# A gated state-space layer: set-up rebuilt, last chunk's outputs by quarters, 16 unused matmuls

## The reference

```python
xn = _layernorm(x)                        # outer norm
x_norm = _layernorm(xn, ln_in_g, ln_in_b) # inner norm
x_norm = x_norm + conv1d(x_norm, conv_w) + conv_b     # depthwise, 3 taps
gate, input_gate = split(x_norm @ gate_w.T + gate_b)
Bm = x_norm * sigmoid(input_gate) @ B_w.T + B_b
Cm = x_norm @ C_w.T + C_b
A_bar = expm(dt_A * A)
s = _layernorm(state @ A_bar + b_t, ln_st_g, ln_st_b) # 2048 times, in order
ssm = (Cm * s) @ D_w.T + D_b
out = x + ssm * sigmoid(gate) * silu(xn @ W.T + b + (xn @ V_r) @ C.T)
```

## Time and profile before

| | us |
|---|---|
| median of 3 runs | 2551.97 (2548.98 to 2552.64) |
| profiled execution, its own time | 2550.3 |
| its span | 2548.5 |
| TensorE busy | 2472.2 (97%) |
| VectorE busy | 2199.2 (86%) |
| GpSimd busy | 1270.9 (50%) |
| ACT busy | 1006.3 (39%) |

### The profile page before, as it was taken

One profiled execution on the slowest core, in us unless ns is written; L12 is line 12 of the kernel. 1 busy time (PEld: TensorE's weight loads), 2 busy tenths in 40 slices (PEclk: granted clock), 3 DMA queues, 4 the chain that ended last, 5 costly groups with the idle time before them and its releaser, 6 DMA issues.

```text
span 2548.5 us, 42474 instructions
## 1 busy us (share of the span) xinstructions
PE 2472.2 (97%) x10001; PEld 1303.5 (51%) x10001; DVE 2199.2 (86%) x10937; ACT 1006.3 (39%) x1834; POOL 1270.9 (50%) x2480
## 2 busy tenths in 40 slices
PE   6899999999999999999999999999999999999986
PEld 3445555555555555555555555555555555555543
DVE  4688898888899888898888899888899888899876
ACT  3343344434344434334444334444344444334310
POOL 1355554455555455555455555455555455555442
PEclk8899999999999999999999999999999999999997
DMA  3111121221121221121222121122111122112112
GB/s 109 24 42 42 40 53 47 54 59 42 40 55 49 51 59 42 40 57 47 51 58 49 40 50 50 47 58 57 38 44 51 49 56 59 41 40 54 31 37 52
DMA packets 99798, 125.19 MB, mean 49 GB/s; under 512 B 32159, under 2 KB 48735, under 8 KB 99552
## 3 DMA queue, kind: packets, MB, share of 16 engines
q1 hardware_dynamic: 98912, 121.43, 19.5%
q10 hardware_dynamic: 640, 1.05, 0.1%
HBM read 71.96 MB, written 33.55 MB: 41 GB/s over the span
## 4 chain that ended last, share of the span: by engine, by line
POOL 48%; DVE 33%; issue 13%; PE 3%; ACT 0%; POOLq 0%; DVEq 0%; DMA 0%; ACTq 0%; SPq 0%
POOL dw L352 43%; DVE wq L760 14%; DVE dw L771 9%; DVE dw L785 9%; POOL ln L374 5%; PE bank L996 1%; PE bank L936 0%; ACT z L422 0%; PE bank L1029 0%; POOLq L223 0%; PE bank L987 0%; POOL ln L376 0%; PE bank L1061 0%; POOL ln L378 0%; POOL ln L377 0%
## 5 line engine op out<-in xcount | busy, mean ns | idle before, releaser
L352 POOL TENSOR_TENSOR dw<-q,minus_half 8x1 f32<-8x1 f32 x2048 | 1101.7, 538 | 1185.7 <-DVE wq L760 1154.9
L1029 PEld LDWEIGHTS bank<-Mscan,wT 128*65 128x65 f32 x2046 | 218.3, 136 | 660.2 <-issue 652.9
L987 PE MATMUL bank<-xnorm,gateT 128*128 128x512 f32 x1024 | 508.2, 595 | 0.0
L760 DVE SCALAR_TENSOR_TENSOR wq<-dw 8x65 f32<-8x65 f32 x2048 | 443.7, 217 | 70.3
L996 PE MATMUL bank<-xnorm,gateT 128*128 128x512 f32 x1024 | 502.7, 598 | 1.1 <-issue 1.1
L979 PE MATMUL bank<-xnT,WT 128*128 128x512 f32 x1024 | 495.7, 595 | 0.0
L1029 PE MATMUL bank<-Mscan,wT 128*65 128x128 f32 x2046 | 408.3, 281 | 33.3 <-DVE wT L788 24.9
L1030 PE MATMUL bank<-Mscan,wT 128*65 128x128 f32 x2046 | 393.3, 274 | 0.0
L785 DVE SCALAR_TENSOR_TENSOR dw<-dw 8x64 f32<-8x64 f32 x1024 | 280.1, 273 | 121.3 <-POOL dw L352 90.6
L771 DVE SCALAR_TENSOR_TENSOR dw<-dw 8x64 f32<-8x64 f32 x1024 | 281.1, 275 | 89.9 <-POOL dw L352 82.7
L775 DVE SCALAR_TENSOR_TENSOR dw<-bank,dw 8x128 f32<-8x128 f32 x1024 | 342.7, 335 | 8.9 <-PE bank L1030 8.0
(11 more groups left out here) (140 smaller groups left out, 2745.9 us busy)
## 6 DMA issues: line engine op xcount, KB each, us to landing
xc<-in_x SPq DMA_DIRECT2D x264, 128.0 KB, 2.7
out<-o SPq DMA_DIRECT2D x256, 128.0 KB, 2.4
xa<-in_x SPq DMA_DIRECT2D x248, 128.0 KB, 2.7
dw<-dtok SPq DMA_DIRECT2D x128, 96.0 KB
wtok<-dw SPq DMA_DIRECT2D x128, 33.0 KB
gateT<-in_gateT SPq DMA_DIRECT2D x1, 2048.0 KB
xa<-in_x ACTq DMA_DIRECT2D x8, 128.0 KB, 3.7
WT<-in_WT SPq DMA_DIRECT2D x1, 1024.0 KB, 6.0
```

The source lines that it names most:

```text
L352: nc.gpsimd.tensor_tensor(dw[0:B, t, CR:CR + 1], q[:], minus_half[0:B, 0:1], ALU.pow).then_inc(s["r_ready"], 1)
L760: V.scalar_tensor_tensor(out=wq[:], in0=w_eps, scalar=1.0 / S, in1=w_eps, op0=ALU.mult, op1=ALU.mult, accum_out=q[:]).then_inc(s["q_ready" ...
L987: ins = mm(mbank["gate", m][:], gateT[:, k, P * m:P * m + P], xnorm[p][:, k, :], start=(k == 0), stop=(k == KH - 1))
L1029: mm(scanP[0:WIDE, 0:2 * S], wT[:, 0:WIDE], Mscan[:, 0, :], start=True, stop=False)
```

## The change

Set-up:
- SP loads the edges and chunk 0 of batches 4 to 7 only; ACT loads VT and CrT (the factors of the low-rank product) first and then the edges and chunk 0 of batches 0 to 3.
- TensorE starts with the four W' products, into four banks instead of two; then come 4 matmuls of the identity with itself, and one more behind each of the 12 series matmuls: 16 whose result nobody reads (`keep_busy`).
- VectorE adds W' behind squarings 0 to 3. Other tables are spread anew: halo transposes behind squarings 0 to 3, z of chunk 0 behind 4, 6, 8, 10, taps behind 8 to 15, input gate from 10 on and by k first, with its own banks, x transposes behind 17 and 19. b_proj is behind the last squaring among the matrix products, and c_proj behind `fill_d`.
- The halo's normalised tiles go to o instead of z, so that ACT normalises halo and chunk 0 one behind the other, and then copies the halo. y and the centre tap alternate by k.
- GpSimd's `ln_op` for n < 3 does the four columns' power as one operation (7 and 5 operations instead of 13 and 8).
- The statistics of chunk 1 (n = 2) end behind the set-up's last VectorE copy.

Last chunk (`LAST` = 31): the gate products stand at steps 25 to 40 instead of 30 to 45. Its outputs are made by quarters of 16 time steps (q = 0 to 3): q = 0 to 2 between the steps 42 to 63, q = 3 behind the scan. A quarter has one transpose of w, an affine of 128 columns, `last_states` (128 columns), `last_mm` (4 products of 128 columns), `last_gated` (two halves of two pieces of 128 columns), `last_fill_o` (4 transposes), `last_sum` (two halves) and one DMA of 256 KB. x is loaded again by quarters early in that chunk.

The diff, cut to its core:

```diff
-PE_GATE_LAST = range(30, 46)
-V_G_LAST = (37, 38, 41, 42, 49, 50, 53, 54)
-PE_HALO = (0, 0, 1, 1)
-PE_Z0 = (2, 2, 3, 3)
-PE_WPRIME = (4, 5, 10, 11)
-DVE_WPRIME = (9, 10, 12, 13)
-DVE_CONV = (4, 5, 6, 7)
-PE_IG0 = (8, 8, 9, 9, 10, 10, 11, 11, 12, 12, 13, 13, 14, 14, 15, 15)
-PE_X0 = (10, 10, 12, 12)
-DVE_XG0 = (11, 13, 15, 17)
-DVE_STATS2 = (14, 15, 16, 17)
-PE_B0 = (14, 16, 17, 18)
-PE_C0 = (17, 18, 19, 19)
+PE_GATE_LAST = range(25, 41)
+V_G_LAST = (30, 31, 34, 37, 38, 41, 42, 45)
+LAST = NC - 1
+PE_W_LAST = (42, 43, 53)
+PE_SSM_LAST = (48, 50, 57)
+PE_O_LAST = (52, 54, 61)
+V_YS_LAST = (46, 49, 56)
+V_SG_LAST = (50, 51, 52, 53, 59, 60)
+V_ADD_LAST = (54, 55, 57, 58, 62, 63)
+PE_HALO = (0, 1, 2, 3)
+PE_Z0 = (4, 6, 8, 10)
+DVE_WPRIME = (0, 1, 2, 3)
+DVE_CONV = (8, 10, 12, 14)
+IG0 = tuple((m, k) for k in range(KH) for m in range(3)) + tuple((3, k) for k in range(KH))
+PE_IG0 = (10, 11, 12, 12, 13, 14, 14, 15, 16, 16, 17, 18, 18, 19, 20, 20)
+PE_X0 = (17, 17, 19, 19)
+DVE_XG0 = (18, 19)
+DVE_STATS2 = (17, 18, 19)
...
+            pe.wait_ge(s["vc_in"], 16 * 2)
+            for k in range(KH):
+                mm(wbank[k][:], VT[:, P * k:P * k + P], CrT[:], start=True, stop=True).then_inc(s["wprime_mm"], 1)
             pe.wait_ge(s["consts"], 16 * 4)
+
+            def keep_busy(n):
+                for _ in range(n):
+                    mm(banks[7][:, 0:P], ident[:], ident[:], start=True, stop=True)
+
+            keep_busy(4)
...
                 mm(scanP[0:S, 0:S], As[:, 1, :], XX[:, 0, :], start=True, stop=True
                    ).then_inc(s["pe_setup"], 1)
+                keep_busy(1)
...
+                whole = lambda a, b: g.tensor_tensor(b, a, minus_half[:], ALU.pow)
+                ins = (first + [
+                    lambda: whole(both, rr),
+                    lambda: g.tensor_tensor(bz, nm, rr, ALU.mult),
+                    lambda: whole(a, r1),
+                    lambda: g.tensor_tensor(bx, nm, r1, ALU.mult),
+                ] if n < 3 else first + [
...
+                for m in range(KH):
+                    ins = mm(last_ssm[q][:, P * m:P * (m + 1)], DT[:, P * m:P * (m + 1)], ys[:, P * q:P * (q + 1)],
+                             start=True, stop=True)
+                ins.then_inc(s["last_ssm"], 1)
...
+            def send_last(q):
+                wait_for(sp, "last_add", 2, q, 2)
+                hold(sp)
+                sp.dma_start(out[:, CT * LAST + QT * q:CT * LAST + QT * (q + 1), :], z[:, q, :]
+                             ).then_inc(s["last_out"], 16)
...
-            iteration(NC, "C", False)
+            send_last(0)
+            send_last(1)
+            send_w(LAST, NQ - 1)
+            send_last(2)
+            send_last(3)
```

More of the change, by code:

```diff
@@ L239, in wait_bank, with load_ends, quarter, of_rows @@
                     return
+        def load_ends(eng, b):
+            p0 = CT * (b % BJ)
+            ends = x[b, :, :].rearrange("(m r) h -> m r h", r=CT)[:, 0:CT:CT - 1, :]
+            eng.dma_start(xc[p0:p0 + CT, b // BJ, :], ends).then_inc(s["halo_in"], 16)
+        def quarter(a, q):
+            return a.rearrange("p (b q t) -> p q b t", b=B, q=NQ)[:, q]
+        def of_rows(a):
+            return a.rearrange("p (b t) -> p b t", b=B)
+        last_p = LAST % 2
+        last_w = [banks[5 + q % 2] for q in range(NQ)]
+        last_ssm = [banks[4 + 3 * (q % 2)] for q in range(NQ)]
+        last_o = [banks[1 + q % 2] for q in range(NQ)]
         block = ctx.enter_context(nc.Block())
@@ L525, in state_affine @@
                 a_(bank, bank, ACT.Identity, bias=sm("st_b"), scale=sm("st_g")).then_inc(s["sn_done"], 1)
-            for b in range(B):
+            for dst, src in [(VT[:], VT_d), (CrT[:], CrT_d)]:
+                act.dma_start(dst, src).then_inc(s["vc_in"], 16)
+            for b in range(B // 2):
+                load_ends(act, b)
+            for b in range(B // 2):
                 p0 = CT * (b % BJ)
@@ L628, in _ @@
             iteration(NC - 1, 1, "FC")
-            iteration(NC, 0, "C")
+            for q in range(NQ):
+                if q == 0:
+                    wait_for(act, "wrfill", 1, LAST, 0)
+                wait_for(act, W_IN[q], 16, LAST, 16)
+                a_(wr[:, q, 0:S], wtok[:, q, CD:CD + S], ACT.Copy,
+                   scale=wtok[:, q, CR:CR + 1]).then_inc(s["last_wr"], 1)
+                wait_for(act, "last_wT", 1, q, 1)
+                bank = last_w[q][0:S, 0:P]
+                a_(bank, bank, ACT.Identity, bias=sm("st_b"), scale=sm("st_g")).then_inc(s["last_sn"], 1)
         @block.vector
@@ L878, in _ @@
             assert done[0] == SETUP_M
+            for h in range(2):
+                gated_x(0, 2, h, 0)
             dve.wait_ge(s["pe_setup"], SQ_END + 1)
@@ L885, in _ @@
             link(V.tensor_copy(dw[0:B, CT - 1, CM:CM2], scanP[0:B, 3 * S:4 * S]))
+            for h in range(2):
+                gated_x(0, 3, h, 0)
             dve.wait_ge(s["pe_setup"], SQ_END + 2)
@@ L890, in _ @@
             assert done[0] == SETUP_END
+            for h in range(2):
+                bn_stats(2, NJ - 1, h)
+            aggregate(2)
             def iteration(i, p, parts):
@@ L923, in _ @@
             iteration(NC - 1, 1, "FC")
-            iteration(NC, 0, "C")
+            last_states(3)
+            for h in range(2):
+                last_gated(3, h)
+            for h in range(2):
+                last_sum(3, h)
         @block.tensor
@@ L1099, in _ @@
             pe.wait_ge(s["dve_setup"], SETUP_END)
+            for k in range(KH):
+                c_proj(0, k, 0, -1, False)
             def iteration(i, p, parts, middle):
```

196 lines of the change are left out of this document (141 added, 55 removed).

## The result

| | before | after |
|---|---|---|
| median | 2550.92 (2548.98 to 2552.64, 4 runs) | 2531.85 (2531.44 to 2532.26, 4 runs) |
| ratio, 95% interval | | 0.9923 (0.991 to 0.9936) |
| profiled span | 2548.5 | 2529.6 |
| mean granted clock | 0.985 | 0.994 |

The sum is close because its terms missed in both directions, which is luck. I cut both profiled executions at the same four points: the scan's first step, the start of chunk 31, the end of the last power, the end of the span.

The account below looks back on a forecast made before the run. The prediction took the serial chain over GpSimd's power and VectorE as the bound. Set-up -15.5, first steps +1.5, last chunk +1.0 and tail -8.4 gave -21.4 us on the median 2551.97: 2530.6 us, range 2520 to 2541.

Parts of the forecast that it names:

- Set-up, -15.5: Before the scan: its first step was to come at 75.5 us instead of 90.98, 15.5 us earlier.
- so I let it rise inside the third product, at 9 to 10: Set-up: TensorE's clock was to rise to 2.4 GHz within the third W' product, at 9 to 10 us.
- I cost them at nothing: Set-up series: the other 12 unused matmuls were to hide in TensorE's 0.43 us waits; uncovered they would cost 3 us.
- The page against the row: Set-up: the skill's page keeps squarings 0 to 10 slow, as forecast; a row's clock rise at 28 allows them fast.
- First steps, +1.5: Scan's first steps: VectorE waiting for the look-ahead was to lose 3.5 us instead of 2.0, costing 1.5 (0 to 4).
- Last chunk, +1.0: Last chunk: earlier gates save 2.2 us, outputs by quarters add more; plus 1.0 in all (-1.5 to +3).
- plus 3.2 for the outputs by quarters: Last chunk: 2.0 us of VectorE pieces, 2.2 of TensorE products, transposes and fills, 0.2 more, less 1.2 for overlap and clock.
- Tail, -8.4: Behind the last power: 9.4 us of computing plus 3.3 for the output DMA, 12.7 instead of 21.1; minus 8.4.
- (a): Unused matmuls and early W' keep TensorE at 2.4 GHz through series, halo fills and gates; 2525 us, chance 0.20.
- (b): Set-up: ACT's serial run and late statistics bind, scan starts at 82, first steps lose 5; 2538.6 us, chance 0.25.
- (c): Set-up: unused matmuls do nothing or cost their 3 us uncovered; 2533 us, chance within the forecast's 0.50.
- (d): GpSimd's 128x4 power, four times in series, makes it slower than before from 6.9 us on; chance 0.02.

Follow-up runs that it names:

- e1: The changed kernel without its 16 unused matmuls; 2526.91 us, ratio 0.9921.
- e4: The changed kernel with the set-up's 128x4 powers as four 128x1 operations each; 2530.98 us, one time only.
- e3: The kernel before with only the new last chunk and tail; 2542.93 us, ratio 0.9969.
- e12: The kernel before with only the last chunk's gates moved earlier (TensorE steps 25 to 40, VectorE 30 to 45); 2550.36 us, ratio 0.9989.
- e2: The changed kernel's set-up with the old last chunk and old tail; 2538.79 us, ratio 0.9961.
- e10: The changed kernel run again without an edit; 2531.69 us, ratio 0.9923.
- e6: The changed kernel without unused matmuls and with W' formed over 128 rows, zero-padded, instead of 32; 2524.92 us, one time only.
- e11: The changed kernel with two unused products behind each series term instead of one; 2539.55 us, ratio 0.9953.
- e8: The changed kernel without the set-up's unused matmuls, with three of 128x512 behind the scan's last look-ahead; 2524.59 us, one time only.
- e7: The changed kernel without the set-up's unused matmuls, with three of 128x512 behind c_proj; 2527.37 us, one time only.
- e9: The changed kernel without its 16 unused matmuls, W' over 128 rows, wide products behind c_proj and in the tail, last output in two halves; 2526.09 us, ratio 0.9899.
- e5: The changed kernel with its first four unused matmuls 512 columns wide, moving ones; 2535.59 us, one time only.

## Why the prediction was right in its sum and wrong in its terms

**Set-up, -15.5 against -9.6.** The step that failed is "so I let it rise inside the third product, at 9 to 10". W' ran for 7.2 us at the lower level, and the four unused matmuls took 2.08 instead of 1, so the series' first operation came at 12.39; that part cost little (12 had been forecast), since the loads landed at 3.26 and not at 5. The following sentence, "I cost them at nothing", is the larger miss: at 1.2 GHz an unused product with its load outlasts the 0.43 us of cover, and made a term 0.22 longer. The series went from 15.29 to 28.91, 13.6 us against 11.2 in e1, and ended 2.4 us behind the 26.5 of the forecast.

The 5.9 us add up like this. When the gates began 3.6 of them were there (46.08 instead of 42.5): the 2.4 of the series; 0.3 from its end to squaring 4 (7.3 us where 7.0 had been forecast, since squarings 0 to 3 took 1.66 each where I had 1.2, while the stall of 2 us at squaring 4 wasn't there: the fill at 36.85 stands right behind the squaring's passes); and 0.9 in squarings 4 to 10, which took 9.85. There the forecast's own terms give 9.85 and not 9: three squarings of 1.07 and four of 0.68 with a fill of 0.98, which hides their wait. The gate products and x's transposes took 22.8 us (to 68.92) where 21.1 had been added up. Their part at the lower clock, 4.3 us, was not longer than forecast. From there to the end of dtok's first copy (76.33) it was 7.4, where 7.5 had been forecast, and the DMA from that copy's end to the first step took 5.1 us where 4.4 had been read the earlier trace rows; SP's wait and issue are in both. The wide power, 1.04 instead of 1.5, was not on this path (e4).

**The page against the row.** The squarings 0 to 10 ran slow (0.47 and 1.11 for four transposes, until 46). The Trainium skill, "TensorE: Matmul & The Clock Gate", Part 4: PE-mode transpose, says that transposes don't engage full speed; here the trace agrees. The rise at 28 in the kernel before speaks against that rule as a general one. It stands in all three traces with the old set-up (28.3, and 29.2 and 28.8 in e3 and e12), which has eight transposes in a row where the new one has four, and no run here shows whether that is the reason.

**First steps, +1.5 against -2.5.** The order was read rightly: chunk 1's transposes do stand before the look-ahead. Two sizes were wrong. ACT's z ended 2.2 us behind the scan's start in the forecast (77.7 against 75.5) and 1.1 behind it in the trace (82.5 against 81.41). And the forecast had no term for the clock, which was still full there: c_proj (76.30 to 79.9), moved right in front of that gap, had run at the higher level. This isn't firm: e2, with the same set-up, took 78.34 for chunk 0, after and e10 76.29 and 76.45. That c_proj as such keeps the clock up is therefore not shown, only that VectorE waits 0.5 to 0.8 us for the look-ahead of step 2 with the clock up (six traces) and 1.9 to 2.4 with it down (e1, e2, e6, e11).

**Chunks 1 to 30.** They took 2.3 us longer without any edit. The powers had a mean of 541 ns against 538 before. e4, with the same middle chunks, had 538 again and 2278.1 us for the 30 chunks. Over all 14 traces, the four with a mean of 538 or 539 (before, e4, e6, e8) took 2278.1 to 2279.9, the ten with 540 or 541 took 2280.6 to 2282.4, the old set-up standing in both groups. So this goes with the execution, not with the change. Per chunk it is 0.08 us, so the 76.1 of the forecast held.

**Last chunk, +1.0 against -2.1.** The minus 2.2 for the wait was right (2.3 in e12). The plus 3.2 for the outputs by quarters came out as 0.25 in this execution and as up to 1.6 in others. Its parts don't close either: the VectorE pieces named are 6.0 us of work, and how they become 2.0 isn't said, and the 0.2 for the fills of w is counted twice. The 1.0 us at step 57 for TensorE's products was rightly seen, but it depends on the clock: the wait came where the clock had fallen by then (0.78 to 1.39 in e1, e3, e7, e9, e11), while in the changed kernel the clock was full from 2501 to 2511 and the longest wait was 0.35. I had also added VectorE's pieces to its steps one by one, but a step of the scan waits for GpSimd's power each time, and a short piece goes into that wait. The timeline of VectorE in the changed kernel shows two quarter pieces, a ys of 0.27 with 0.19 of wait left behind it and a sum of 0.41, in a pair of steps that took 2508.22 - 2505.85 = 2.37 us, no more than any other:

```profile
2505.85 0.27 DVE L871 SCALAR_TENSOR_TENSOR dw<-dw 8x64 f32<-8x64 f32 x1
...
2506.57 0.27 DVE L833 TENSOR_TENSOR ys<-bank,cT 64x128 f32<-64x128 f32 x1
2507.03 0.27 DVE L885 SCALAR_TENSOR_TENSOR dw<-dw 8x64 f32<-8x64 f32 x1 [0.19 <-POOL dw L401]
...
2507.82 0.41 DVE L855 TENSOR_TENSOR z<-bank,xa 128x256 f32<-128x256 f32 x1
2508.22 0.27 DVE L871 SCALAR_TENSOR_TENSOR dw<-dw 8x64 f32<-8x64 f32 x1
```

**Tail, -8.4 against -7.1.** The computing part was forecast at 9.4 and took 9.42, operation by operation. The output was under-sized: 4.6 us for one DMA of 256 KB where I took 3.3 from one of 128 KB. It was within the bounds (to 5), and e9 took 3.5 by halves.

**The rivals.** (a) did not happen, the clock stayed low. (b) named the right place for the wrong reason: the scan did start at 81.4, near its 82, but TensorE's series was late, not ACT; e4 shows ACT and GpSimd with 1.1 us to spare on the way to the scan's start. (c), the unused matmuls uncovered, is what happened; they cost 4.4 us to the gates' start and not 3, because the price had been worked out for the higher clock. (d) did not happen: the wide power took 1.04 us.

## What to carry to other kernels

- A filler matmul costs what it costs at the clock that it finds. Compare it, with its weight load and at the lower level, with the wait that it is to fill before calling it free, and look in the trace whether the operations behind it got shorter.
- If the clock is to be raised, look which products it rose behind here: 512 columns over all 128 rows (e5, e6, e9), and not 512 columns over 32 rows nor 128 columns of the identity (with the old set-up it rose behind transposes, too). Then look whether anything behind them still ran at the higher clock: in all three it was down again at the series' first term.
- Before a difference of a few us between two traces is put down to an edit, compare several traces with the same code: one set-up started the scan at 76.17, 76.78 and 78.48 by the moment at which the clock rose.
- In a serial scan, extra pieces are to be priced against the waits of the engine that carries them, not summed; and a late product in front of a serial step is worth more than all of them, so first look where the longest single wait is, and at which clock that product may run.
